# Projections of a cross-attention layer: 192 features cut 128 + 64 instead of 96 + 96, and one factor per row for x's norms

## What is computed

```python
def stable_layernorm(x, g):
    x = x / jnp.max(x, axis=-1, keepdims=True)
    mean = jnp.mean(x, axis=-1, keepdims=True)
    var = jnp.var(x, axis=-1, keepdims=True)
    return (x - mean) * jax.lax.rsqrt(var + EPS) * g
...
x = stable_layernorm(_layernorm(x), g_norm)
q = x @ Wq                               # 256 -> 512, 8 heads of 64
k, v = split(context @ Wkv)              # 192 -> 512 each
q = l2norm(q) * q_scale                  # per head
k = l2norm(k) * k_scale
sim = q @ k.T * 8.0
```

## Time and profile before

| | |
|---|---|
| timed runs | 797.54, 796.9, 794.32 us; median 796.9 |
| profiled execution | span 799.0 us (its only time), mean granted clock of TensorE 0.941 |
| busy in the span | TensorE 702.9 us, VectorE 372.2, ScalarE 413.8, POOL 253.4 |
| layer 2's projections | about 323 to 444 us, a period of 14.0 us for each batch |

### The profile page before, as it was taken

The page is one execution under the profiler, slowest core; times in us unless marked ns, Lnnn a source line. Parts: engine busy times, 40 slices in busy tenths (PEclk is TensorE's granted clock), DMA queues, the critical chain, the costliest instruction groups (busy, mean ns, idle before and its releaser), DMA issues.

```text
span 799.0 us, 15926 instructions
## 1 busy us (share of the span) xinstructions
PE 702.9 (88%) x4979; PEld 569.5 (71%) x4980; DVE 372.2 (47%) x1126; ACT 413.8 (52%) x966; POOL 253.4 (32%) x322
## 2 busy tenths in 40 slices
PE   3997999997539999699999899986799999999995
PEld 2775666665438898477666566655479999999995
DVE  4223577776421111476777555556843434242432
ACT  2445789987313332355556878763234444444442
POOL 5112455553160000211211000001236666666652
PEclk9998799999559999899999999996899999999999
DMA  5126000000835971100100100000044443344431
GB/s 134 42 82 199 1 2 2 2 3 1 295 119 182 301 247 33 54 24 19 38 19 0 46 2 1 2 1 1 0 132 131 129 120 122 121 122 120 129 112 41
DMA packets 58549, 62.51 MB, mean 78 GB/s; under 512 B 5920, under 2 KB 51206, under 8 KB 58378
## 3 DMA queue, kind: packets, MB, share of 16 engines
q1 hardware_dynamic: 55530, 58.40, 23.6%
q10 hardware_dynamic: 1952, 1.91, 0.8%
q0 software_dynamic: 1024, 1.64, 0.7%
HBM read 54.72 MB, written 7.22 MB: 78 GB/s over the span
## 4 chain that ended last, share of the span: by engine, by line
PE 68%; DVE 11%; ACT 9%; issue 5%; DMA 3%; POOL 3%; SPq 1%; DVEq 0%; POOLq 0%; ACTq 0%
PE psum L1876 6%; PE psum L1878 6%; PE psum L1877 5%; ACT probs L697 4%; PE psum L1040 4%; PE psum L1053 3%; PE psum L1395 3%; PE psum L1891 3%; PE psum L1892 3%; PE psum L545 3%; PE psum L1890 3%; PE psum L559 3%; PE psum L1416 3%; PE psum L636 3%; PE psum L1403 2%
## 5 line engine op out<-in xcount | busy, mean ns | idle before, releaser
L2000 DVE TENSOR_TENSOR kT_all<-kT_all 128x400 f32<-128x400 f32 x60 | 36.6, 611 | 114.5 <-ACT kT_all L1934 106.5
L1973 POOL TENSOR_TENSOR h_low<-v_all,h_high 128x400 fp32r<-128x400 f32 x60 | 63.1, 1051 | 65.5 <-ACT h_high L1938 65.4
L1876 PE MATMUL psum<-xT_high,we_high 128*128 128x400 f32 x240 | 83.3, 347 | 0.0
L1878 PE MATMUL psum<-xT_high,we_low 128*128 128x400 f32 x240 | 82.8, 345 | 0.0
L1877 PE MATMUL psum<-xT_low,we_high 128*128 128x400 f32 x240 | 82.5, 344 | 0.0
L697 ACT ACTIVATE probs<-probs,negmax 100x361 f32<-100x361 f32 x128 | 68.9, 587 | 10.8 <-POOL probs L742 10.7
L1964 POOL TENSOR_TENSOR we_low<-v_all,we_high 128x512 fp32r<-128x512 f32 (+1 forms) x61 | 66.6, 1101 | 19.6 <-ACT we_high L1923 16.0
L750 DVE TENSOR_SCALAR_CACHE_REDUCE probs<-psum 100x361 f32<-100x361 f32 x128 | 60.7, 531 | 19.5 <-PE psum L626 19.5
L636 PEld LDWEIGHTS psum<-ident,probs 100*128 100x128 f32 (+1 forms) x384 | 40.2, 159 | 27.6 <-issue 19.8
L636 PE MATMUL psum<-ident,probs 100*128 100x100 f32 (+1 forms) x384 | 48.7, 266 | 11.1 <-ACT probsT L705 4.8
L1934 ACT ACTIVATE kT_all<-psum 128x400 f32<-128x400 f32 x60 | 30.0, 501 | 52.7 <-PE psum L1878 52.7
(11 more groups left out here) (350 smaller groups left out, 1566.7 us busy)
## 6 DMA issues: line engine op xcount, KB each, us to landing
v_all<-in_L_ffn_W_dram SPq DMA_DIRECT2D x16, 1024.0 KB, 7.7
kT_all<-coefT_dram SPq DMA_DIRECT2D x30, 400.0 KB, 3.5
v_all<-in_L_ffn_Wg_dram SPq DMA_DIRECT2D x31, 128.0 KB, 2.1
v_all<-in_L_ffn_Wu_dram SPq DMA_DIRECT2D x31, 128.0 KB, 2.2
v_all<-in_L_ffn_Wd_dram SPq DMA_DIRECT2D x31, 128.0 KB, 2.1
ctx_nat<-in_ctx_dram SPq DMA_DIRECT2D x17, 192.0 KB, 2.5
xs_dram<-zeros SPq DMA_DIRECT2D x1, 2048.0 KB, 7.7
ys_dram<-zeros SPq DMA_DIRECT2D x1, 1792.0 KB, 12.5
```

The source lines that it names most:

```text
L1876: nc.tensor.matmul(ps, we_high[p][:, col], xT_high[:, c, tok], start=(c == 0), stop=False)
L1878: last = nc.tensor.matmul(ps, we_low[p][:, col], xT_high[:, c, tok], start=False, stop=(c == 1))
L1973: nc.gpsimd.tensor_tensor(h1_low[p][:, tok], h1T[:, tok], h1_high[p][:, tok].bitcast(F32), ALU.subtract).then_inc(h1_ready, 1)
```

## The change

The 192 features are contracted as 128 + 64 rows. The context is kept with its last 64 features twice (features 128 to 191 also in columns 192 to 255), so that the transpose puts them on partitions 0 to 63 and 64 to 127; the last 64 rows of Wk and Wv are likewise loaded on both halves. `times` becomes `first_rows` (three products over 128 rows) and `rest_rows` (three products over 64 rows for each tile; with two tiles in a call, tile 0 on the lower half of the array and tile 1 on the upper one, alternating, into different banks). Keys: first 0, first 1, rest of 0 and 1, first 2, rest of 2. Values: first 0; q's transposes and products; first 1, rest of 0 and 1 (this raises `v1_in_psum` by two), then, after `v1_stored`, first 2 and rest 2.

The two norms and the division become (x - mean) * g and a factor per row, rstd = 1 / sqrt(EPS * (max - mean)^2 + var), which enters q's squares as their scale and q's scaling through one more multiplication of `q_ss`. ScalarE has one Sqrt for it instead of two. ScalarE's order is otherwise as before.

```diff
+DREST = DC - 128
...
-    ctx_nat = [sb(f"ctx_nat{p}", [P, 3, DC], F32) for p in range(2)]
+    ctx_nat = [sb(f"ctx_nat{p}", [P, 3, 2 * P], F32) for p in range(2)]
...
-    wk1, wv1 = (two(vals_arena[:, 6 * SLOT_V + k * 1024:])[0:DCC] for k in range(2))
+    wk1, wv1 = (two(vals_arena[:, 6 * SLOT_V + k * 1024:]) for k in range(2))
...
-    ctxT_full = nc.alloc_sbuf_tensor_at("ctxT_full", [DCC, 2, NKV], F32, offset=qm_at + 4 * 1024 * 4)
+    ctxT_full = nc.alloc_sbuf_tensor_at("ctxT_full", [P, 2, NKV], F32, offset=qm_at + 4 * 1024 * 4)
...
+    ctxT1_ps = psum[:, 0:2, 0:NKV]
...
+    def sp_ctx1(sp, b, p):
+
+        sp_ctx(sp, b, p)
+        src = a["ctx_768"][b][:, P:DC]
+        sp.dma_start(ctx_nat[p][:, 0:FULL, DC:2 * P], src[0:FULL * P, :].rearrange("(t p) d -> p t d", p=P)
+                     ).then_inc(ctx_loaded[p], 16)
+        sp.dma_start(ctx_nat[p][0:TAIL, FULL, DC:2 * P], src[FULL * P:NKV, :]).then_inc(ctx_loaded[p], 16)
...
-        pe.wait_ge(ctx_loaded[p], 32 * (B // 2 + 1 - p) + loaded)
-        for c in range(2):
-            for t in range(3):
-                last = nc.tensor.transpose(ctxT_ps[:, c, t * P:t * P + rows[t]],
-                                           ctx_nat[p][0:rows[t], t, c * DCC:(c + 1) * DCC],
-                                           ident[0:rows[t], 0:rows[t]])
+        pe.wait_ge(ctx_loaded[p], 32 * (B // 2 + 1 - p) + 2 * loaded)
+        for t in range(3):
+            cols = slice(t * P, t * P + rows[t])
+            nc.tensor.transpose(ctxT1_ps[:, 0, cols], ctx_nat[p][0:rows[t], t, 0:P], ident[0:rows[t], 0:rows[t]])
+            last = nc.tensor.transpose(ctxT1_ps[:, 1, cols], ctx_nat[p][0:rows[t], t, P:2 * P], ident[0:rows[t], 0:rows[t]])
...
-            sp_ctx(sp, p, p)
-        wkv = a["L1_xattn_Wkv"].rearrange("(c p) n -> p c n", p=DCC)
-        sp.dma_start(wk1, wkv[:, :, 0:512]).then_inc(w1x_loaded, 16)
-        sp.dma_start(wv1, wkv[:, :, 512:1024]).then_inc(w1x_loaded, 16)
+            sp_ctx1(sp, p, p)
+        for w, at in ((wk1, 0), (wv1, 512)):
+            src = a["L1_xattn_Wkv"][:, at:at + 512]
+            sp.dma_start(w[:, 0, :], src[0:P, :]).then_inc(w1x_loaded, 16)
+            for k in range(2):
+                sp.dma_start(w[k * DREST:(k + 1) * DREST, 1, :], src[P:DC, :]).then_inc(w1x_loaded, 16)
...
+        sp.wait_ge(w1x_split, 2)
...
-        act.wait_ge(w1x_loaded, 48)
+        act.wait_ge(w1x_loaded, 16 * 7)
...
-                def spread():
-
-                    chain(nc.vector.memset(turn[:, 0:1], 0.0), wait=False)
-                    nc.vector.bn_aggr(mv[:, 0, :], stats[:, 0, :]).then_inc(ln_stats, 1)
-
-
+                mean = mv[:, 0, 0:1]
                 dve.wait_ge(y_gathered[p], 16 * i + 16)
                 chain(nc.vector.scalar_tensor_tensor(y_row, y_tok[:, p, :], top_weight[:, bass.ds(b, 1)], x[:, b + 1, :],
                                                      ALU.mult, ALU.add))
+                chain(nc.vector.tensor_reduce(row_max[:, 0:1], y_row, AX.X, ALU.max), wait=False)
                 chain(nc.vector.bn_stats(stats[:, 0, :], y_row), wait=False)
                 nc.vector.tensor_copy(x[:, b + 1, :], y_row).then_inc(x2_added, 1)
                 dve.wait_ge(x2_step, X2_STEPS * b + count[0])
-                spread()
-                dve.wait_ge(ln_std, 3 + 2 * b + 1)
-                chain(nc.vector.reciprocal(rstd[:, 0:1], std[:, 0:1]))
-                chain(nc.vector.tensor_scalar(y_row, y_row, mv[:, 0, 0:1], rstd[:, 0:1], ALU.subtract, ALU.mult))
-                chain(nc.vector.tensor_reduce(row_max[:, 0:1], y_row, AX.X, ALU.max))
-                chain(nc.vector.reciprocal(row_max[:, 0:1], row_max[:, 0:1]))
-                chain(nc.vector.tensor_scalar(y_row, y_row, row_max[:, 0:1], None, ALU.mult))
-                chain(nc.vector.bn_stats(stats[:, 0, :], y_row))
-                spread()
-                dve.wait_ge(ln_std, 3 + 2 * b + 2)
-                chain(nc.vector.reciprocal(rstd[:, 0:1], std[:, 0:1]))
-                chain(nc.vector.tensor_scalar(y_row, y_row, mv[:, 0, 0:1], rstd[:, 0:1], ALU.subtract, ALU.mult))
+                chain(nc.vector.memset(turn[:, 0:1], 0.0), wait=False)
+                chain(nc.vector.bn_aggr(mv[:, 0, :], stats[:, 0, :]))
                 dve.wait_ge(xnT_in_psum, 2 * B + b)
-                nc.vector.tensor_tensor(xn[:, :], y_row, g_norm[:, :], ALU.mult).then_inc(xn_ready, 1)
+                nc.vector.scalar_tensor_tensor(xn[:, :], y_row, mean, g_norm[:, :], ALU.subtract, ALU.mult
+                                               ).then_inc(xn_ready, 1)
+                chain(nc.vector.tensor_scalar(row_max[:, 0:1], row_max[:, 0:1], mean, None, ALU.subtract))
+                nc.vector.tensor_tensor(row_max[:, 0:1], row_max[:, 0:1], row_max[:, 0:1], ALU.mult).then_inc(ln_stats, 1)
                 dve.wait_ge(xnT_in_psum, 2 * B + b + 1)
                 nc.vector.tensor_copy(xnT[:, :, :], xnT1_ps).then_inc(xnT_ready, 1)
+                dve.wait_ge(ln_std, 3 + b + 1)
+                nc.vector.reciprocal(rstd[:, 0:1], std[:, 0:1]).then_inc(q1_factor, 1)
...
+                chain(nc.vector.tensor_scalar(q_ss[:, :], q_ss[:, :], rstd[:, 0:1], None, ALU.mult))
...
-    X2_STEPS = 12
+    X2_STEPS = 7
 
     def pe_project1(pe):
-        def times(p, ps, t, high, low):
-
-            for c in range(2):
-                cols = slice(t * P, t * P + rows[t])
-                nc.tensor.matmul(ps, ctxT_high[p][:, c, cols], high[:, c, :], start=(c == 0), stop=False)
-                nc.tensor.matmul(ps, ctxT_high[p][:, c, cols], low[:, c, :], start=False, stop=False)
-                last = nc.tensor.matmul(ps, ctxT_low[p][:, c, cols], high[:, c, :], start=False, stop=(c == 1))
+        def first_rows(p, ps, t, high, low):
+
+            cols = slice(t * P, t * P + rows[t])
+            nc.tensor.matmul(ps, ctxT_high[p][:, 0, cols], high[:, 0, :], start=True, stop=False)
+            nc.tensor.matmul(ps, ctxT_high[p][:, 0, cols], low[:, 0, :], start=False, stop=False)
+            nc.tensor.matmul(ps, ctxT_low[p][:, 0, cols], high[:, 0, :], start=False, stop=False)
+
+        def rest_rows(p, tiles, high, low):
+
+            for x_part, w_part in ((ctxT_high[p], high), (ctxT_high[p], low), (ctxT_low[p], high)):
+                for k, (ps, t) in enumerate(tiles):
+                    at = slice(k * DREST, (k + 1) * DREST)
+                    last = nc.tensor.matmul(ps, x_part[at, 1, t * P:t * P + rows[t]], w_part[at, 1, :],
+                                            start=False, stop=(x_part is ctxT_low[p]))
             return last
 
         pe.wait_ge(w1x_split, 2)
@@ -1303,17 +1310,18 @@
                 b = 2 * i + p
 
                 pe.wait_ge(ctxT_split, b + 1)
-                for t in range(3):
+                keys = [(k1_ps[0:rows[t], t, :], t) for t in range(3)]
+                for ps, t in keys:
                     pe.wait_ge(kT1_stored, 3 * b + t + 1)
-                    last = times(p, k1_ps[0:rows[t], t, :], t, wk1_high, wk1_low)
-                last.then_inc(k1_in_psum, 1)
-
-                def values(t):
-                    times(p, v1_ps[t][0:rows[t], :], t, wv1_high, wv1_low).then_inc(v1_in_psum, 1)
+                    first_rows(p, ps, t, wk1_high, wk1_low)
+                    if t == 1:
+                        rest_rows(p, keys[0:2], wk1_high, wk1_low)
+                rest_rows(p, keys[2:3], wk1_high, wk1_low).then_inc(k1_in_psum, 1)
 
                 pe.wait_ge(experts_taken, 1)
                 transpose_ctx1(pe, 1 - p, 32 * i + 32 * (p + 1))
-                values(0)
+                values = [(v1_ps[t][0:rows[t], :], t) for t in range(3)]
+                first_rows(p, *values[0], wv1_high, wv1_low)
 
                 pe.wait_ge(xn_ready, 2 * B + b + 1)
                 pe.wait_ge(qT1_stored, b + 1)
@@ -1325,9 +1333,11 @@
                 for c in range(2):
                     last = nc.tensor.matmul(q1_ps[0:NQ, :], xnT[:, c, :], wq1[:, c, :], start=(c == 0), stop=(c == 1))
                 last.then_inc(q1_in_psum, 1)
-                values(1)
+                first_rows(p, *values[1], wv1_high, wv1_low)
+                rest_rows(p, values[0:2], wv1_high, wv1_low).then_inc(v1_in_psum, 2)
                 pe.wait_ge(v1_stored, 3 * b + 1)
-                values(2)
+                first_rows(p, *values[2], wv1_high, wv1_low)
+                rest_rows(p, values[2:3], wv1_high, wv1_low).then_inc(v1_in_psum, 1)
...
-                for k in range(2):
-                    act.wait_ge(ln_stats, 2 * B + 2 * b + k + 1)
-                    nc.scalar.activation(std[:, 0:1], mv[:, 0, 1:2], ACT.Sqrt, bias=eps_col[0:NQ, :]).then_inc(ln_std, 1)
+                act.wait_ge(ln_stats, 2 * B + b + 1)
+                nc.scalar.activation(std[:, 0:1], row_max[:, 0:1], ACT.Sqrt, bias=mv[:, 0, 1:2], scale=EPS).then_inc(ln_std, 1)
...
-                nc.scalar.activation(o_tok[:, :], q1_ps[0:NQ, :], ACT.Square).then_inc(q1_squared, 1)
```

(30 more changed lines are left out.)

10 lines of the change are left out of this document (2 added, 8 removed).

## The result

| | before | changed |
|---|---|---|
| four timed runs each, us | 794.32 to 797.54, median 796.41 | 814.54 to 821.58, median 820.15 |
| profiled execution: span, clock | 799.0 us, 0.941 | 817.6 us, 0.940 |
| TensorE, VectorE, ScalarE busy | 702.9, 372.2, 413.8 us | 708.2, 358.3, 411.0 us |

The ratio is 1.0287, 95% interval [1.0265, 1.031]: slower by 23.7 us between medians, 18.6 between the profiled executions. The forecast said slower, 808.0, with a range to 821; the forecast's own range ended at 813.

What follows compares the result with a forecast made beforehand. TensorE, nearly full, and VectorE alternate as the bound in layer 2's projections. Six periods +10.2, last batch +1.6, batch 0 -1.5, loads +0.5 make +10.8: span 809.8, median 807.7, given as 808, range 800 to 821.

Steps and rivals of the forecast that it cites:

- the gain arrives: Rival at ScalarE's copy of v tile 0: it does not hold up the key root; period 13.58, time 792.3; chance 0.08.
- they cancel: Rival: the wait is about half a microsecond rather than 2.2 and the gain pays it; 797; chance 0.08.
- pairs do not overlap: Rival in TensorE's 64-row products: keys and paired values each +0.69 per batch, 11.0 more, 818.7; chance 0.11.
- The clock falls: Rival: TensorE's longer waits bring it to 1.2 GHz in some batches; in three batches 10 more, 818; chance 0.13.
- Product slot and pair, 0.23: TensorE's key and value products: a 512-column product takes 0.231 us, an overlapping 64-row pair 0.23; six fewer slots per batch.
- Change of form, 0.10: TensorE going into or out of half-array form: 0.10 us each, bounds 0 and 0.20; eight per batch, five on the path.
- New wait: ScalarE's copy of v tile 0 waits for the paired values; key root at 10.28, 1.50 later; period 15.80, +1.70.
- Second wait: TensorE waits about 0.9 before tile 2's values for tile 0's copy; hidden, since it waits 1.8 before q transposes.
- Batch 0, -1.5: First batch of layer 2's projections, where xn is waited for: batch 1 starts 2.5 or 0.4 earlier, 1.5 taken.
- Norms in a steady batch: VectorE and ScalarE: removed norm work saves nothing; the new reciprocal adds 0.16, the multiplication by rstd 0.20.
- Loads, +0.5: SP's eight more loads ahead of the expert weights start those some 4 us later; bounds 0 and 2, 0.5 taken.

Runs made afterwards that it cites:

- e1_copy_later: Changed kernel with ScalarE's copy of v tile 0 moved behind the root of key_ss and the Square of q: 799.4 us, 1.0017 of the kernel before.
- e2_wait_alone: Kernel before, with v tile 0's values counted complete only with tile 1's, all else as before: 821.19 us, 1.0302.
- e4_one_half: Changed kernel with both tiles' 64-row products on the lower half of the array, so no pair can overlap: 829.78 us, 1.0401 of the kernel before.
- e6_filled_waits: Changed kernel with idle TensorE products, two before the wait for v1_stored, five before that for the scaled q: 812.11 us, 1.0193 of the kernel before.
- e3_norms_alone: Kernel before, with only the one factor per row in place of two norms and a division: 799.28 us, 1.0035.
- e5_other_pairs: Changed kernel with pairs key 0 with key 1, key 2 with value 0, value 1 with value 2: 801.3 us, 1.0049 of the kernel before.
- e7_no_factor: e5_other_pairs without the factor per row (maximum, root, reciprocal and multiplication of q_ss left out): 801.79 us, 1.0059 of the kernel before.
- e9_two_inputs: e5_other_pairs with VectorE's guard of the key norms written as an instruction reading the same tile twice: 801.48 us, 1.0057 of the kernel before.
- e8_pool_later: e5_other_pairs with POOL's context subtraction moved behind the inversion of the key roots: 791.41 us, 0.9912 of the kernel before.

## Why the prediction was right, and twice too small

The mechanism was the forecast's: tile 0's copy waits for the pairs, and the key root waits behind the copy. e1_copy_later (undone: 14.15) and e2_wait_alone (made alone: 16.44) show it from both sides. Against the rivals: "the gain arrives" and "they cancel" fell with 10.59 for the root; "pairs do not overlap" fell with the 0.23 from pair to pair and with e4_one_half. "The clock falls" came true, not in place of the forecast but on top of it. So the range held with some luck: 820.15 lies 7 us above the forecast's own range (802 to 813) and 1 us inside the full one, which reached so far only for the rivals.

- **Product slot and pair, 0.23.** Right: 0.23 for both.
- **Change of form, 0.10.** Mis-sized. The step into another form costs 0.33 - 0.23 = 0.10 (394.55 to 394.88), and the first product in the new form holds its follower another 0.10 (394.88 to 395.21, or 395.77 to 396.09), so nearly the upper bound of 0.20. Up to the xn transposes that made 5.62 rather than 5.41, and 0.08 more in the paired values. The price read from the earlier trace rows was half of that. The Trainium skill's statement (TensorEngine Tiling (Array Packing), "Key Properties") that changing the tiling mode drains the engine fits in kind. The drain of about 128 cycles that the prediction took from the Trainium skill's TensorE: Matmul & The Clock Gate ("Part 2: What happens when you issue a matmul"), by its estimate 0.05 us, would be a quarter of what is measured.
- **New wait.** Root at 10.59 (forecast 10.28), q scaled 4.26 after the root (4.21), q transposes 0.74 after that, as forecast: at 15.59 in the batch where 15.23 was forecast. The next keys follow 0.35 later in this batch and 0.57 in the one before (392.73 to 393.30), the kind that the forecast was made for: that batch 3 takes 16.16 from key to key (377.14 to 393.30) where 15.80 was forecast, +2.06 and not +1.70. All of the 0.36 is named: 0.21 and 0.08 from the changes of form, 0.05 in VectorE's chain, the rest rounding.
- **Second wait.** TensorE stood 0.78 before tile 2's values (forecast 0.9) and 1.61 to 1.66 before the q transposes (1.8); hidden, as forecast.
- **Clock.** Three of seven batches at 17.5 to 17.7: 52.85 us against 3 x 16.04, so 4.7 us. The prediction priced such a batch at up to 3.5 and left it out of the sum. e6_filled_waits measures the term: its periods take 4.5 us less, though the medians differ by 8. The error here is of kind: the clock's fall was made a rival of the wait (0.13), though it is a consequence of it, as the filled waits show. The sum held only the direct part.
- **Batch 0, -1.5.** From VectorE's addition to the q transposes it gained 0.27 (15.26 to 14.99). The norms alone gave 3.3 (e3_norms_alone) and the xn transposes did come 3.4 earlier; the wait for the pairs ate the rest, and the half clock stands in this batch (0.83 from 320 to 340). The half clock, 10.2 us long before (331.8 to 342.2), is 6.8 us long after (329.8 to 336.8). The pricing by the steady batch missed over a microsecond.
- **Norms in a steady batch.** Right: what goes saved nothing there, and what comes costs 0.34 a batch by itself (e3_norms_alone), where the prediction had 0.16 and 0.20. In e3_norms_alone gain and cost nearly balance (1.0035).
- **Loads, +0.5.** Cost nothing: first expert product 1.8 earlier.

By the spans: forecast +10.8; measured +18.6. The wait with its changes of form is 7 x (16.04 - 13.98) = 14.4 of it and the clock 4.5, together the +18.94 of the seven periods; ahead of them the changed kernel is 1.7 earlier (343.22 for 344.95), behind them 1.4 slower (357.6 for 356.2), which is less than that part differs between profiled executions. The medians differ by 5 more than the spans: the changed kernel's profiled execution took 819.37 us, 1.8 more than its span, so that of before, with the same 1.8, ran about 4 long of its median. Where, no run shows.

Which of the two waits brings the clock down is in part to be read from the traces. All 13 falls between the first and the last q transposes of these kernels (three in the changed kernel, four in e2_wait_alone, one in e4_one_half, two in e5_other_pairs, one in e7_no_factor, two in e9_two_inputs) begin within 1.6 us of the start of q transposes, and e5, e7 and e9 have no wait for tile 0's copy. So the wait for the scaled q is enough; filling it alone in the changed kernel was not tried.

Open: why some batches fall and others with the same wait do not; why e2_wait_alone fell in four batches with waits of 1.42 us, where the changed kernel has 1.66 and fell in three, and e8_pool_later with 1.22 to 1.29 in none; and why the fall in e4_one_half lasts 10.2 us, three times as long as those of the changed kernel.

## To carry to other kernels

Work finished later is paid for at the head of the queue that takes it, not where it is used: before pairing or delaying a product, look at what stands behind its consumer. Here the consumer (a value copy) was in no hurry, and the small root behind it was on the path; moving one line removes the loss, and so does another partner for the pair, once POOL's subtraction is out of the guard's way. When a stage becomes faster, look again at which instructions now fall together in time, even those of engines off the path.
